# Local attention with the values product one tile later, and the norm behind it spread over two neighbouring blocks

## The reference, cut to what matters

```python
x = L0_attn_a_hidden_states                       # (16, 1024, 256)
x = x + _L0_attn_a_ref(_layernorm(x), w_qkv, b_qkv)      # local attention
x = x + _L0_ffn_ref(_layernorm(x), ...)                  # feed-forward f1: the norm in question is "n2"
x = x + _L0_attn_b_ref(_layernorm(x), ...)               # differential attention (most of the time)
x = x + _L0_ffn_ref(_layernorm(x), ...)                  # feed-forward f2
...
# local attention: 16 heads of 16, softmax over groups of 32 tokens (half groups of 64)
out1 = _attention(q1, k1, v1, d)
# feed-forward: a global net on the mean over tokens, and three cycles of a coupling net
global_context = x.mean(axis=1, keepdims=True)
gf = _global_net(global_context, ...)
for _ in range(NUM_CYCLES):
    tf = _coupling_net(out, ...)                  # layers 1 to 4, gelu between them
    out = out + coupling * _twist(out)
```

## Time and profile before

| what | value |
|---|---|
| median of 3 runs | 7971.05 us (7957.34 to 7980.41) |
| the profiled execution, its own time | 7964.95 us |
| its span, first to last instruction | 7963.3 us |
| PE busy, whole span | 7373.2 us (93%) |
| DVE busy | 6889.1 us (87%) |
| ACT busy | 6124.5 us (77%) |
| POOL busy | 3628.6 us (46%) |

### The profile page before, as it was taken

The page is one execution under the profiler, slowest core; times in us unless marked ns, Lnnn a source line. Parts: engine busy times, 40 slices in busy tenths (PEclk is TensorE's granted clock), DMA queues, the critical chain, the costliest instruction groups (busy, mean ns, idle before and its releaser), DMA issues. The chain is left out here.

```text
span 7963.3 us, 182322 instructions
## 1 busy us (share of the span) xinstructions
PE 7373.2 (93%) x72640; PEld 3328.7 (42%) x72640; DVE 6889.1 (87%) x8962; ACT 6124.5 (77%) x11390; POOL 3628.6 (46%) x5187
## 2 busy tenths in 40 slices
PE   6899988999889998899988999889998999989999
PEld 4344443444434444344443444434444344443444
DVE  5899868997689976899769997699976999769997
ACT  3699756997569975699756997569975699756997
POOL 4366333663336623466234662346613466135661
PEclk9999999999999998999989999999999999999999
DMA  1122102120022100222002220021200222002210
GB/s 32 53 45 44 30 12 56 44 48 24 12 56 48 44 24 12 57 48 44 23 12 59 47 45 24 10 64 44 47 23 5 64 44 48 26 2 64 48 44 26
DMA packets 604400, 298.88 MB, mean 38 GB/s; under 512 B 487094, under 2 KB 528566, under 8 KB 603510
## 3 DMA queue, kind: packets, MB, share of 16 engines
q1 hardware_dynamic: 603516, 286.86, 14.8%
HBM read 123.84 MB, written 67.37 MB: 24 GB/s over the span
## 5 line engine op out<-in xcount | busy, mean ns | idle before, releaser
L1548 DVE TENSOR_REDUCE mall<-ps 128x1 f32<-128x1024 f32 x4096 | 4669.5, 1217 | 71.7 <-PE ps L1482 68.4
L1639 ACT ACTIVATE work<-ps 128x512 f32<-128x512 f32 x8192 | 4311.2, 603 | 164.0 <-PE ps L1498 39.9
L1514 PE MATMUL ps<-work,vbuf 128*32 128x256 f32 x32768 | 2624.3, 392 | 21.6
L1498 PE MATMUL ps<-qop,kop 51*128 51x256 bf16 x16384 | 2558.1, 273 | 10.6 <-ACT work L1639 8.8
L1482 PE MATMUL ps<-kop,qop 48*128 48x512 bf16 x8192 | 2535.4, 384 | 33.6 <-DMA kop<-scratch 18.8
L1498 PEld LDWEIGHTS ps<-qop,kop 51*128 51x128 bf16 x16384 | 1182.0, 94 | 1887.5 <-ACT work L1639 1596.1
L1514 PEld LDWEIGHTS ps<-work,vbuf 128*32 128x32 f32 x32768 | 661.8, 108 | 923.4 <-issue 591.1
L252 POOL TENSOR_TENSOR rstd<-rstd,nhalf 128x8 f32<-128x8 f32 x64 | 109.3, 1707 | 1501.9 <-DVE rstd L246 1501.9
L1573 POOL TENSOR_TENSOR mall<-mall 128x8 f32<-128x8 f32 x1024 | 212.9, 208 | 1254.9 <-DVE mall L1548 1214.8
L444 POOL TENSOR_TENSOR hh<-work,hmask 128x1024 f32<-128x1024 f32 x256 | 516.2, 2045 | 457.0 <-POOLq L1744 362.1
L1601 POOL TENSOR_TENSOR work<-work,none 128x16 f32<-128x16 f32 x224 | 650.4, 2904 | 18.1
(11 more groups left out here) (179 smaller groups left out, 8317.1 us busy)
## 6 DMA issues: line engine op xcount, KB each, us to landing
qop<-scratch SPq DMA_DIRECT2D x512, 64.0 KB
scratch<-work SPq DMA_DIRECT2D x32, 768.0 KB, 4.3
scratch<-hh SPq DMA_DIRECT2D x32, 768.0 KB, 3.8
kop<-scratch SPq DMA_DIRECT2D x256, 96.0 KB
vbuf<-in_x SPq DMA_DIRECT2D x9, 2048.0 KB, 8.4
qop<-scratch SPq DMA_DIRECT2D x512, 32.0 KB
kop<-scratch SPq DMA_DIRECT2D x256, 64.0 KB
qop<-mT SPq DMA_DIRECT2D x1024, 3.0 KB
```

What stands on the lines that cost most here:

```text
L1498: mm = pe.matmul(ps[:, bank, part * HQ:(part + 1) * HQ], kop[r:r + KM, s, i, (t + part) * P:(t + part + 1) * P], qop[r:r + KM, s, i, quart ...
L1514: mm = pe.matmul(ps[VW * i:VW * (i + 1), OB, kept], vp[:, b, t, (G * gl + i) // 2, :], prob[:, u % PS, i, cols], start=t == 0, stop=t == T ...
L1548: v.tensor_reduce(mall[:, m // CUT % 2, to, col:col + 1], ps[:, b:b + NB, :].rearrange("p b n -> p (b n)"), AX.X, ALU.max).then_inc(s_mr, 1)
L1639: act.activation(prob[:, u % PS, hl, :], ps[:, EB[slot % len(EB)], :], ACT.Exp, scale=scale).then_inc(s_ex, 1)
```

## The change

Three things move. (1) TensorE takes `values(t - 3)` instead of `values(t - 2)` in its step t, so that its loop has 19 steps instead of 18. (2) The block `layernorm("n2")` is gone. The first sequence's tiles are normalised by VectorE right after its loop in local attention, transposed by TensorE ahead of the last `values` (`first_turns`), and copied to `hT` behind that; the two `regroup` pieces that use the same banks wait for these copies (`s_ld`). (3) The second sequence's norm is done in the feed-forward: `spread` and the root at its start, the transposes after three of the four pieces of `layer1(0)`, the copies on ScalarE and VectorE; the mean over each sequence waits for its copies, and chunk 1 waits for all of them. In both feed-forwards, `global_net(0)` now stands behind both pieces (0, 0) and (0, 1) of `layer1(1)` instead of between them.

```diff
@@ local_attention @@
+                    def first_turns():
+                        for t in range(T):
+                            pe.wait_ge(s_h, t + 1)
+                            for c, bank in enumerate((t // 4, VB + 2 + t // 4)):
+                                mm = pe.transpose(ps[:, bank, t % 4 * P:(t % 4 + 1) * P],
+                                                  h[:, t, c * P:(c + 1) * P], ident[:, :])
+                            mm.then_inc(s_tp, 1)
...
                             pe.wait_ge(s_xs, k + 1)
+                            if k >= 2:
+                                pe.wait_ge(s_ld, k - 1)
...
-                    for t in range(TT + 2):
+                    for t in range(TT + 3):
                         if t < TT:
                             scores(t)
-                        if t >= 2:
-                            values(t - 2)
+                        if t == TT + 3 - 1:
+                            first_turns()
+                        if t >= 3:
+                            values(t - 3)
...
+                    v.wait_ge(norm[2], 1)
+                    for n in range(NB):
+                        normalised(v, n, s_h)
+                    for n in range(NB):
+                        v.wait_ge(s_tp, 4 * (n + 1))
+                        v.tensor_copy(hT[:, 0, 1, half(n)], ps[:, VB + 2 + n, :]).then_inc(s_ld, 1)
                     for k in range(4):
                         residual(1, k)
...
+                    for n in range(NB):
+                        act.wait_ge(s_tp, 4 * (n + 1))
+                        act.copy(hT[:, 0, 0, half(n)], ps[:, n, :]).then_inc(s_lc, 1)
@@ ffn @@
-                    layer1(0)
-                    layer1(1, ((0, 0),))
+                    if second_norm:
+                        layer1(0, ((0, 0), (0, 1), (1, 0)))
+                        for t in range(T, TT):
+                            norm_turned(pe, t, s_h0, s_tp0)
+                        layer1(0, ((1, 1),))
+                        pe.wait_ge(s_lc, CH)
+                        pe.wait_ge(s_ld, CH)
+                    else:
+                        layer1(0)
+                    layer1(1, ((0, 0), (0, 1)))
                     global_net(0)
-                    layer1(1, ((0, 1),))
                     layer2(0, 0)
...
+                    def second_copy(n):
+                        b, cols = chunk_of(n)
+                        act.wait_ge(s_tp0, 4 * (n + 1))
+                        act.copy(hT[:, b, 0, cols], ps[:, 4 * b + n % NB, :]).then_inc(s_lc, 1)
...
                     layer1(0)
-                    layer1(1, (0,))
+                    if second_norm:
+                        for n in range(NB, CH):
+                            second_copy(n)
+                    layer1(1)
                     global_net(0)
-                    layer1(1, (1,))
...
+                    def mean(b):
+                        if second_norm:
+                            v.wait_ge(s_lc, NB * (b + 1))
+                            v.wait_ge(s_ld, NB * (b + 1))
                         v.tensor_reduce(gm[:, :, b], hT[:, b, :, :], AX.X, ALU.add).then_inc(s_gm, 1)
+
+                    if second_norm:
+                        spread(v, norm0, 1)
+                    mean(0)
+                    if second_norm:
+                        v.wait_ge(norm0[2], 2)
+                        for n in range(NB, CH):
+                            normalised(v, n, s_h0)
+                        for n in range(NB, CH):
+                            second_keep(n)
+                    mean(1)
                     keep(0)
...
+                    if second_norm:
+                        root(pool, norm0, 1)
@@ the loop @@
-            local_attention(n2)
-            layernorm("n2", n2)
+            n2_turn = [sem(f"n2_{n}") for n in ("h", "tp", "lc", "ld")]
+            local_attention(n2, *n2_turn)
...
-            ffn("f1", n3, ahead=n3_ahead, first_unit=lambda pe: project[0](pe, first_unit=True))
+            ffn("f1", n3, ahead=n3_ahead, first_unit=lambda pe: project[0](pe, first_unit=True),
+                second_norm=[n2] + n2_turn)
```

More of the change, by code:

```diff
@@ L252, in root, with normalised @@
             pool.tensor_tensor(rstd[:, sequence], rstd[:, sequence], nhalf[:, sequence], ALU.pow).then_inc(s_rs, 1)
+        def normalised(v, n, s_h):
+            for t in range(4 * n, 4 * n + 4):
+                v.tensor_scalar(h[:, t, :], x[:, t, :], mv[:, t, 0:1], rstd[:, t:t + 1],
+                                ALU.subtract, ALU.mult).then_inc(s_h, 1)
         def norm_turned(pe, t, s_h, s_tp):
@@ L268, in _ @@
                 def _(v):
[L269 to L272, removed]
                     def keep(n):
@@ L285, in _ @@
                                 v.wait_ge(norm[2], n // NB + 1)
-                            normalised(n)
+                            normalised(v, n, s_h)
                         if n > N0:
@@ L304, in _, with local_attention @@
                         act.copy(hT[:, b, 0, cols], ps[:, 4 * b + n % NB, :])
-        def local_attention(norm):
+        def local_attention(norm, s_h, s_tp, s_lc, s_ld):
             qkT = work[:, 0:8 * N].rearrange("p (b m n) -> p b m n", b=PB, m=4)
@@ L619, in both, with ffn @@
             return shared[name]
-        def ffn(tag, norm, q=None, ahead=None, first_unit=None, following=None):
+        def ffn(tag, norm, q=None, ahead=None, first_unit=None, following=None, second_norm=None):
+            if second_norm:
+                norm0, s_h0, s_tp0, s_lc, s_ld = second_norm
             if following:
@@ L1006, in keep, with second_keep @@
                             v.tensor_copy(V[n][:, m, :], ps[:, first_bank(n) + 2 + m, :]).then_inc(s_ev, 1)
-                    for b in range(PB):
-                        v.tensor_reduce(gm[:, :, b], hT[:, b, :, :], AX.X, ALU.add).then_inc(s_gm, 1)
+                    def second_keep(n):
+                        b, cols = chunk_of(n)
+                        v.wait_ge(s_tp0, 4 * (n + 1))
+                        v.tensor_copy(hT[:, b, 1, cols], ps[:, 4 * b + NB + n % NB, :]).then_inc(s_ld, 1)
+                    def mean(b):
+                        if second_norm:
+                            v.wait_ge(s_lc, NB * (b + 1))
+                            v.wait_ge(s_ld, NB * (b + 1))
+                        v.tensor_reduce(gm[:, :, b], hT[:, b, :, :], AX.X, ALU.add).then_inc(s_gm, 1)
+                    if second_norm:
[8 more added lines that the diff above has]
+                    mean(1)
                     keep(0)
@@ L1318, in inverse_root, with scaled @@
             pool.tensor_tensor(rr[:, j, :], sv[:, j, :], nhalf[:, 0:HV], ALU.pow).then_inc(s_pw, 1)
-        def normalised(eng, g, side, by, root):
+        def scaled(eng, g, side, by, root):
             b, cols = g // NG, slice(g % NG * 2 * LD, (g % NG + 1) * 2 * LD)
@@ L1327, in normalise @@
             v.wait_ge(s_pw, j + 1)
-            normalised(v, FIRST + j // 2, j % 2, diff[j % 3], rr[:, j, :]).then_inc(s_an, 1)
+            scaled(v, FIRST + j // 2, j % 2, diff[j % 3], rr[:, j, :]).then_inc(s_an, 1)
         def diff_attention(project_pe, project_values, project_dve, project_pool, project_act, project_done,
@@ L1614, in early_rest @@
                         link(pool.tensor_tensor(err, esv, nhalf[:, 0:HV], ALU.pow))
-                        link(normalised(pool, j // 2, j % 2, ediff, err))
+                        link(scaled(pool, j // 2, j % 2, ediff, err))
                     project_pool(pool, cut)
```

## The result

The changed kernel takes 7879.1 us in the median of 4 runs (7868.84 to 7897.36), the kernel before 7966.18 us beside it: a ratio of 0.9892, 95% interval 0.9867 to 0.9916, so 1.1% faster, 87 us. The forecast was 7890 (7855 to 7940). The profiled execution has a span of 7878.7 us, 84.6 less than the earlier trace rows.

What follows compares the result with a forecast made beforehand. It took a hold by PE's waiting values on DVE and POOL as the bound, then DVE, then the drain and norm block. 6.5 - 0.8 + 4.2 = 9.9 us a pass, 79 for eight, gave 7890 us (7855 to 7940).

Steps and rivals of the forecast that it cites:

- Part 1: Local attention's tiles: values three tiles behind removes the hold on DVE and POOL, 6.5 us a pass gained.
- The ceiling of part 1: Local attention: at most DVE's idle time for scores between tile 6 and its last turn, 7.6 us a pass.
- the head's 2.2 us: Local attention's first steps: scores(3) and all behind it come about 2.2 us earlier, counted within the 7.6 us ceiling.
- The last 14% should cost little: Local attention: POOL going from 86% busy to full should hardly slow DVE's multiply L486, 0.72 us in the median.
- The slower rival: POOL without pauses drags DVE's L486 and its like: 118 us slower, 8088; decides at 0.62 us more a tile; chance 0.03.
- Part 2: Drain of local attention: with the first sequence's norm there, values(15) starts 0.8 us later; DVE pays nothing.
- Part 3: Second sequence's norm in f1, one block end less: 4.2 us a pass gained, 6.5 at full clock.
- Part 4: Global net one piece later in f1 and f2: 0 us.
- Another hold: Local attention: ACT's step or POOL replaces the hold, Part 1 gives 0 to 3 us: 39 us in all, 7932; chance 0.15.
- a sign of being wrong: Local attention: POOL or ACT standing at 95% with DVE still waiting would show the prediction wrong.
- The clock stays up: Clock stays up in f1 and the tiles' pace reaches all of the ceiling: 106 us, 7865; chance 0.12.

Runs made afterwards that it cites:

- lag_only: The kernel before with only values three tiles behind the scores instead of two: 7899.6 us, ratio 0.9913.
- fill_all: The change with filler identity transposes on PE in the drain, behind the last regroup and ahead of differential attention's first maximum product: 7829.9 us, ratio 0.9819.
- fill_f1: The change with 16 filler transposes of the identity on PE behind the last regroup, before the feed-forward: 7862.84 us, ratio 0.9855.
- gn_between: The change with global_net(0) again between the two first pieces of layer1(1) in both feed-forwards: 7872.73 us, ratio 0.9897.
- pool_light: The change with GpSimd masking only 16 of 128 key columns from tile 8 on, so the result is not the reference's: 7867.93 us in one run.
- fill_da: The change with only 12 filler identity transposes in PE's wait for differential attention's first key operands: 7847.8 us, ratio 0.9854.
- norm_only: The change with values two tiles behind as before, so only the norm spread over drain and feed-forward: 7964.85 us, ratio 0.9990.
- before_fill_da: The kernel before with 12 filler identity transposes in PE's wait for differential attention's first key operands: 7965.63 us, ratio 0.9998.

## Why the prediction was right, point by point

The sum, 9.9 us a pass and 79 in all, met 84.6 in the spans and 87 in the medians. The mechanisms of parts 1 and 3 are shown, but that the number fits so well is partly luck. Parts 1 to 3 measure 8.7 - 0.7 + 5.1 = 13.1 us a pass, 105 in all; two terms were too small, and the 3.2 us that differential attention took back, of which the prediction knows nothing, brought the sum down to the forecast.

The range has a slip: 8 to 12 us a pass are 64 to 96 in all, from the median 7875 to 7907, and not 7870 to 7912.

- **Part 1, 6.5 us.** The mechanism is shown by lag_only. The size was 8.7. In the pass that I read it was 6.9 (89.89 to 82.95), near the forecast; but that pass was not the usual one. Six of the eight passes of before took 92.6 us and more. The first of them loses it ahead of `scores(6)`; in the other five the clock fell behind PE's long wait (timeline of PE, and two stretches, of before's third pass):

```profile
2102.34 1.08 PE L392 MATMUL ps<-vbuf,work 128*32 128x128 f32 x32 [3.40 <-ACT vbuf L548]
2103.35 2.08 PE L410 MATMUL ps<-ident,hh 128*64 128x64 f32 x32
2105.36 1.94 PE L376 MATMUL ps<-hh,work 128*32 128x256 f32 x16
```

```profile
2102.29:2104.29 2.00, 1.95 (x48) 1.76 (x50) 1.97 (x4) 1.27 (x3) 2.00 (x2) 0.98 0.00 0
2104.29:2106.29 2.00, 2.00 (x32) 1.42 (x34) 0.15 (x1) 1.93 (x4) 0.59 (x1) 0.50 0.00 0
```

  A `scores` takes 1.94 us there and 1.07 elsewhere. Little of the 2.8 us that such a pass loses is DVE's waiting, though: from `scores(6)` on DVE idles 7.9 us in the third pass and 7.2 in the second. It is busy 46.40 us instead of 44.31, and the multiplies of tiles 5 to 15 take 10.39 instead of 8.23. With PE late, DVE's multiplies of tiles 11 and 12 fell early in POOL's pieces and had to wait for their end (the two rows of tile 11 above). With the long wait in the tiles gone, the passes of the change lie between 82.95 and 84.31. Reading one pass of eight hid this.
- **The ceiling of part 1** was wrong too, in the step that took the head's 2.2 us for "the first of these waits seen from the other side". They are separate. In the second pass `scores(6)` stood 38.40 us behind the first `kx` before and stands 35.48 behind it now, 2.9 us; from there to the last turn it was 51.5 us, of which DVE idled 7.2, and is 47.47, of which DVE idles 2.1. That is 2.9 and 4.0, and the ceiling was the sum of both waits, about 10. DVE's idle time fell by 5.1 us; the stretch gained 4.0, since DVE's busy time in it rose by 1.1.
- **"The last 14% should cost little"** argued from POOL's share, and that is not what the multiply's time follows: what counts is where in a piece of POOL's it begins. Its mean went from 0.845 to 1.004 us, 2.5 us a pass over 16 tiles, but 2.1 of these are in tiles 0, 2 and 3, in the head. They can cost time only there, and there the passes of the change differ by no more than 1.4 us (35.48 to 36.84 us from the first `kx` to `scores(6)`); from `scores(6)` on all of them take the same 47.47 us. In tiles 5 to 15 the multiplies take 9.87 us in the change, 8.23 in the pass that I read, and 9.57 in the mean of before's eight passes. So against the pass that I read POOL's company took back part of the gain, and against the mean only 0.3 us. The 8.7 are 2.8 us ahead of `scores(6)` and 5.9 behind it, where DVE's idle time fell from a mean of 7.7 us to 2.1: more than the ceiling, because it was set too low, and because most passes were slower than the one read. The slower rival's mechanism is real, at 0.16 us a tile where 0.62 would have decided.
- **Part 2, 0.8 us later.** 0.73 in the mean, but 0.1 to 1.3 by pass. DVE and ACT paid nothing, as said. PE's transposes ran at 0.23 us each at the lower clock, not at DVE's pace; fill_all, at full clock, has the start 0.5 us earlier than before.
- **Part 3, 4.2 us.** 5.1 measured. The clock was low as said, and cost 1.7 us in the second pass and 2.0 in the mean against fill_f1, where I had taken 2.3. The pieces themselves took 12.5 us and not 13.0: I had added durations, and back-to-back groups overlap by 0.1 to 0.2 us each. No added wait was on the path: in the second pass DVE's second mean ended 1.9 us before `global_net(0)` (1160.33 against 1162.19), and so in the other seven.
- **Part 4, nothing.** 0.1 us by gn_between. But it gives the second mean 1.7 us more room.
- **The rivals.** Another hold did not come: POOL's share went to 96%, which was a sign of being wrong, but by pool_light its pace costs nothing. "The clock stays up" came true in one pass of eight of the change's first trace, in two of its second, in four of fill_da's, and in all where f1 had fillers. What no rival had is the give-back: 3.2 us a pass in this pair of traces, in a stage that the change does not touch. The two traces of before have no loss of 7 us in 16 passes, lag_only two in 8, norm_only four in 8, so most of it goes with the spread norm. That the loss is the clock's, in this wait, is shown by fill_da, and that the kernel before hardly has it by before_fill_da; that the wait's 0.4 us more is what makes the clock fall fits the counts above and is not shown by a run of its own; why the key operands' issue comes 0.5 us later behind the second write to `scratch` with the spread norm is open. Its own instructions are the same; what differs is the program around it and the state that the stages leave. No run separates the two.

## What to carry to other kernels

When an in-order engine waits for a product of the previous tile, look at what stands behind the waiting instruction: the cost is there, and one more tile of lag, where the buffers allow it, removes it without any new work. Then read every pass, not one, since a wait of about 3 us on TensorE may or may not drop its clock, and count such waits as a risk of their own: a change that saves work elsewhere can lengthen one. Dummy transposes in such waits, 66 a pass, were worth 49 us here, more than half of what the change itself brought. And where VectorE's two-input instructions run beside GpSimd's, don't ask how full GpSimd is, but where in one of its instructions they begin.

## What the runs showed of the hardware

- A drop of the granted clock to 0.50 behind a wait of 2.89 us lasted some 34 us in differential attention, with PE busy for most of it, and the pass took 7 us more; behind one of 4.06 us in fill_f1 the clock was back at 1.00 after some 3.5 us, and in f1 it was back about 4 us after PE had started. The Trainium skill, "TensorE: Matmul & The Clock Gate", Part 1, says that activity releases the throttle; f1 agrees with that; the 34 us at the start of differential attention, where PE was busy at the lower clock, do not. No run here tells why.
- A VectorE multiply of 128x512 with two SBUF inputs that began during a GpSimd multiply of 128x1024 (1.90 us) ended 0.55 us behind the end of that one, and took 0.68 to 2.35 us; beside a GpSimd memset it took 0.68. Its mean was 0.845 us before and 1.004 in the change. The Trainium skill, "GPSIMD Engine Reference", section 1, names this contention; the size is this case's.
